# The low-rank tile of a mixture-of-experts kernel: six matmuls and two gelus, or four matmuls and one

## The reference

```
h = gelu(buf @ w1 + b1);  y = h @ w2 + b2          # 256 -> 1024 -> 256
a = gelu(buf @ wd) @ wu                            # 256 -> 32 -> 256, the low-rank branch
y = y + a                                          # weighted, added to the token's row
sh = gelu(xt @ sw1 + sb1) @ sw2 + sb2 + gelu(xt @ swd) @ swu     # shared expert, all tokens
out = out + 0.2 * sh
```

## Time and profile before

| | |
|---|---|
| median of three runs | 178.74 us (177.51 to 179.64) |
| the profiled execution | 177.45 us, span 175.6 us |
| TensorE matmuls busy | 169.9 us, 97%, 1442 matmuls |
| VectorE busy | 144.1 us, 82% |
| ScalarE busy | 140.5 us, 80% |
| GpSimd busy | 96.8 us, 55% |
| chain that ended last | TensorE 93%, DMA 5% |
| mean granted clock of TensorE | 0.999 |

### The profile page before, as it was taken

One profiled execution on the slowest core, in us unless ns is written; L12 is line 12 of the kernel. 1 busy time (PEld: TensorE's weight loads), 2 busy tenths in 40 slices (PEclk: granted clock), 3 DMA queues, 4 the chain that ended last, 5 costly groups with the idle time before them and its releaser, 6 DMA issues.

```text
span 175.6 us, 4118 instructions
## 1 busy us (share of the span) xinstructions
PE 169.9 (97%) x1442; PEld 164.3 (94%) x1442; DVE 144.1 (82%) x330; ACT 140.5 (80%) x315; POOL 96.8 (55%) x112
## 2 busy tenths in 40 slices
PE   5799999999999999999999999999999999999994
PEld 5666879999999999999999999999999999999993
DVE  3478999998695889989889699798988989889722
ACT  3277789407888998997899799999899999897920
POOL 5835348511547572097678858868837555074700
PEclk9999999999999999999999999999999999999999
DMA  4599100069929484595987768769778598776242
GB/s 127 163 350 349 41 2 4 7 175 299 362 56 318 103 304 111 194 252 79 307 252 117 275 193 157 213 197 234 194 255 185 144 312 164 247 247 78 30 90 67
DMA packets 25981, 31.84 MB, mean 181 GB/s; under 512 B 4668, under 2 KB 22488, under 8 KB 25960
## 3 DMA queue, kind: packets, MB, share of 16 engines
q1 hardware_dynamic: 21816, 26.22, 46.7%
q0 software_dynamic: 3904, 5.25, 17.0%
q10 hardware_dynamic: 240, 0.10, 0.2%
HBM read 26.31 MB, written 5.24 MB: 180 GB/s over the span
## 4 chain that ended last, share of the span: by engine, by line
PE 93%; DMA 5%; SPq 0%; DVE 0%; issue 0%; DVEq 0%
PE y_ps L1056 14%; PE y_ps L1057 14%; PE y_ps L1058 14%; PE hid_ps L1056 10%; PE hid_ps L1057 10%; PE hid_ps L1058 10%; DMA x_in<-in_x 5%; PE turn_ps L1056 4%; PE turn_ps L1058 4%; PE turn_ps L1057 4%; PE turn_ps L1235 3%; PE row_ps L1251 1%; PE hid_ps L1095 1%; PE y_ps L1195 1%; PE y_ps L1215 1%; PE y_ps L1251 0%
## 5 line engine op out<-in xcount | busy, mean ns | idle before, releaser
L495 POOL DMA_INDIRECT out_rows<-y_row,slot_tok x23 | 38.5, 1675 | 26.8 <-DVE y_row L946 11.6
L481 POOL DMA_INDIRECT slot_in<-slot_rows,slot_src x23 | 29.5, 1281 | 17.0 <-issue 6.1
L1056 PE MATMUL y_ps<-w_h,hid_h 128*128 128x256 f32 (+2 forms) x128 | 36.4, 285 | 0.0
L1057 PE MATMUL y_ps<-w_l,hid_h 128*128 128x256 f32 (+2 forms) x128 | 36.1, 282 | 0.0
L1058 PE MATMUL y_ps<-w_h,hid_l 128*128 128x256 f32 (+2 forms) x128 | 36.1, 282 | 0.0
L741 DVE TENSOR_TENSOR hid_l<-gelu_f,hid_h 128x320 fp32r<-128x320 f32 (+3 forms) x54 | 26.5, 500 | 8.0 <-ACT hid_h L643 7.5
L1056 PE MATMUL hid_ps<-xs_h,w_h 128*128 128x248 f32 (+6 forms) x96 | 27.6, 288 | 0.0
L1058 PE MATMUL hid_ps<-xs_h,w_l 128*128 128x248 f32 (+6 forms) x96 | 27.2, 284 | 0.0
L1057 PE MATMUL hid_ps<-xs_l,w_h 128*128 128x248 f32 (+6 forms) x96 | 27.2, 284 | 0.0
L718 DVE TENSOR_TENSOR w_l<-w_raw,w_h 128x512 fp32r<-128x512 f32 x40 | 26.7, 703 | 0.0
L643 ACT ACTIVATE hid_h<-hid_ps,bias_s 128x320 fp32r<-128x320 f32 (+2 forms) x48 | 26.4, 549 | 0.0
(11 more groups left out here) (260 smaller groups left out, 465.9 us busy)
## 6 DMA issues: line engine op xcount, KB each, us to landing
w_raw<-in_L_ffn_w SPq DMA_DIRECT2D x16, 1024.0 KB
w_raw<-in_L_ffn_sw SPq DMA_DIRECT2D x3, 1024.0 KB
x_in<-in_x SPq DMA_DIRECT2D x2, 512.0 KB, 4.1
w_raw<-in_L_ffn_sw SPq DMA_DIRECT2D x2, 512.0 KB, 6.5
slot_rows<-token_row SPq DMA_DIRECT2D x8, 128.0 KB, 5.1
wu_raw<-in_L_ffn_wu SPq DMA_DIRECT2D x24, 32.0 KB
out_rows<-base SPq DMA_DIRECT2D x1, 512.0 KB
slot_in<-slot_rows,slot_src POOLq DMA_INDIRECT x23
```

Source lines behind the costliest of these rows:

```text
L481: pool.indirect_dma_start(out=slot_in[par][0:n, s, :], out_offset=None, in_=x_rows, in_offset=bass.IndirectOffsetOnAxis(ap=slot_src[0:n, e ...
L495: pool.indirect_dma_start(out=out, out_offset=bass.IndirectOffsetOnAxis(ap=slot_tok[0:n, e, s:s + 1].bitcast(U32), axis=0), in_=y_row[0:n, ...
L1056: pe.matmul(out_ap, l_h, r_h, start=start, stop=False)
L1057: pe.matmul(out_ap, l_h, r_l, start=False, stop=False)
```

## The change

The low-rank tile of the routed experts takes four matmuls. Its stationary operand `wd_s` holds the high part twice and the low part twice (4 x 32 columns), so that each of `xs_h` and `xs_l` passes once for each of the two halves of the inputs; the bank then has the high-part products on partitions 0 to 63 and the low-part products on 64 to 127. ScalarE copies the upper half out (`low_copy`), VectorE adds the two halves (`low_sum`), ScalarE takes one gelu of the sum in float32 (`low_gelu_part`, behind the gelus of tile 2), and VectorE rounds it by a copy and subtracts the rounded from the unrounded for the low part (`low_lo`, behind the split of tile 2).

The tile is moved: for expert 0 it stands where it stood, for the others it is issued inside the last output tile of the expert before, ahead of its last three matmuls (`LOW_MADE_AT`). The bank `turn_ps[0]` is awaited for tile 5 by the sum. The two slot copies of an expert on ScalarE become one over both banks, and so do the two subtractions on VectorE. On GpSimd the wd cast comes ahead of the gathers. The shared expert's low-rank tile is as before.

```diff
-        turn_ps = [bank(f"turn_ps{i}") for i in range(2)]
+        turn_both = ctx.enter_context(nc.psum_tensor("turn_both", [P, KD, 512], F32))
+        turn_ps = [turn_both[:, k, :] for k in range(KD)]
-        wd_h = [sb(f"wd_h{i}", [P, KD, 3, RANK], F32R) for i in range(2)]
-        wd_l = [sb(f"wd_l{i}", [P, KD, 3, RANK], F32R) for i in range(2)]
+        wd_s = [sb(f"wd_s{i}", [P, KD, 4, RANK], F32R) for i in range(2)]
+        low_sums = gelu_f[0:2 * RANK, 0:2, SLOTS:SLOTS + SLOTS // 2]
...
GpSimd:
             def period(e, par):
+                if e + 2 <= E:
+                    wd_hi_part(e + 2, par)
                 if e + 2 < E:
                     gather(e + 2, par)
-                if e + 2 <= E:
-                    wd_hi_part(e + 2, par)
                 wu_hi_part(e + 2, par)
...
ScalarE:
+            def low_copy(e):
+                act.wait_ge(low_made, e + 1)
+                act.activation(low_sums, halves(turn_ps[0][2 * RANK:4 * RANK, 0:SLOTS]), ACT.Copy).then_inc(low_copied, 1)
+            def low_gelu_part(e):
+                act.wait_ge(low_summed, e + 1)
+                act.activation(low_sums, low_sums, ACT.Gelu).then_inc(low_gelu, 1)
             def slots_hi_part(n):
-                for k in range(KD):
-                    act.activation(xs_h[:, k, 0:n], turn_ps[k][:, 0:n], ACT.Copy).then_inc(slots_hi, 1)
+                act.activation(xs_h[:, :, 0:n], turn_both[:, :, 0:n], ACT.Copy).then_inc(slots_hi, 1)
...
-                for j in range(HT):
+                low_copy(e)
+                for j in range(1, HT):
                     gelu_tile(e + 2, j, MOST[e], lambda f: bias_s[:, e, f:f + 1])
+                    if j == LOW_GELU_AT:
+                        low_gelu_part(e)
...
VectorE:
             def slots_lo_part(e):
                 n = MOST[e]
-                for k in range(KD):
-                    dve.wait_ge(slots_hi, e * KD + (k + 1))
-                    dve.tensor_tensor(xs_l[:, k, 0:n], turn_ps[k][:, 0:n], xs_h[:, k, 0:n].bitcast(F32),
-                                      ALU.subtract).then_inc(slots_lo, 1)
+                dve.wait_ge(slots_hi, e + 1)
+                dve.tensor_tensor(xs_l[:, :, 0:n], turn_both[:, :, 0:n], xs_h[:, :, 0:n].bitcast(F32),
+                                  ALU.subtract).then_inc(slots_lo, 1)
...
+            def low_sum(e):
+                dve.wait_ge(low_copied, e + 1)
+                dve.tensor_tensor(low_sums, halves(turn_ps[0][0:2 * RANK, 0:SLOTS]), low_sums, ALU.add).then_inc(low_summed, 1)
+            def low_lo(e):
+                dve.wait_ge(low_gelu, e + 1)
+                if e > 0:
+                    dve.wait_ge(low_used, e)
+                dve.tensor_copy(halves(low_s[0:2 * RANK, 0:SLOTS]), low_sums).then_inc(low_round, 1)
+                dve.wait_ge(low_round, e + 1)
+                dve.tensor_tensor(halves(low_s[2 * RANK:LOW, 0:SLOTS]), low_sums[0:RANK, :, :],
+                                  halves(low_s[0:RANK, 0:SLOTS].bitcast(F32)),
+                                  ALU.subtract).then_inc(low_split, 1)
...
-                for j in range(HT):
+                low_sum(e)
+                for j in range(1, HT):
                     split_tile(e + 2, j, MOST[e])
+                    if j == LOW_GELU_AT:
+                        low_lo(e)
...
TensorE:
+            def low_tile(e, par, size):
+                pe.wait_ge(slots_lo, e + 1)
+                pe.wait_ge(wd_lo, e + 2)
+                for k in range(KD):
+                    both = wd_s[par][:, k, :, :].rearrange("p g r -> p (g r)")
+                    pe.matmul(turn_ps[0][:, 0:size], both, xs_h[:, k, 0:size], start=(k == 0), stop=False)
+                    ins = pe.matmul(turn_ps[0][:, 0:size], both, xs_l[:, k, 0:size], start=False, stop=(k == KD - 1))
+                ins.then_inc(low_made, 1)
...
+                    if m == KD - 1 and f == LOW_MADE_AT:      # expert_out; rows_out likewise in its last tile
+                        midway()
...
-                    pe.wait_ge(slots_lo, (e + 1) * KD)
-                    for j in range(HT):
+                    if e == 0:
+                        low_tile(0, other, size)
+                    for j in range(1, HT):
                         hidden(e + 2, j, other, e + 1, xs_h, xs_l, slice(0, size), size)
```

More of the change, by code:

```diff
@@ L52 @@
 RING = 5
+LOW_GELU_AT = 2
+LOW_MADE_AT = 7
 MOST = [min(SLOTS, K * T // (r + 1)) for r in range(E)]
@@ L249, in build @@
         wu_lo = sem("wu_lo")
+        low_made = sem("low_made")
+        low_copied = sem("low_copied")
+        low_summed = sem("low_summed")
+        low_gelu = sem("low_gelu")
+        low_round = sem("low_round")
+        low_split = sem("low_split")
+        low_used = sem("low_used")
         hid_made = sem("hid_made")
@@ L284, in hid_count @@
         def hid_count(u, j):
-            return u * HT + (j + 1) - (1 if u == LAST else 0)
+            return u * HT + (j + 1) if u < 2 else 2 * HT + (u - 2) * NF + j
         def turned_part(g):
@@ L334, in held_by @@
         def held_by(u, j):
-            tiles = [i for i in range(1 if u == LAST else 0, j) if hid_banks(u)[i] is hid_banks(u)[j]]
+            tiles = [i for i in range(0 if u < 2 else 1, j) if hid_banks(u)[i] is hid_banks(u)[j]]
             return tiles[-1] if tiles else None
@@ L1140, in hidden @@
                     pe.wait_ge(wd_lo, v + 1)
-                if u < 2 and j == 0:
                     return shared_low(u, x_h, x_l, cols, n)
@@ L1144, in hidden @@
                     pe.wait_ge(hid_gelu, hid_count(u, held_by(u, j)))
+                elif 2 <= u < LAST and hid_bank(u, j) is turn_ps[0]:
+                    pe.wait_ge(low_summed, u - 1)
                 elif u == 1:
                     pe.wait_ge(hid_gelu, hid_count(0, HT - 1))
-                m = P if j > 0 else LOW
-                dst = hid_bank(u, j)[0:m, 0:n]
+                dst = hid_bank(u, j)[:, 0:n]
                 for k in range(KD):
-                    if j == 0:
-                        l_h, l_l = (w[:, k, :, :].rearrange("p g r -> p (g r)") for w in (wd_h[par], wd_l[par]))
-                    else:
-                        l_h, l_l = (w[:, k, (j - 1) * P:j * P] for w in (w1_h[par], w1_l[par]))
+                    l_h, l_l = (w[:, k, (j - 1) * P:j * P] for w in (w1_h[par], w1_l[par]))
                     ins = three(dst, l_h, l_l, x_h[:, k, cols], x_l[:, k, cols], k == 0, k == KD - 1)
@@ L1180, in shared_out, with expert_out @@
                 ins.then_inc(y_made, 1)
-            def expert_out(e, m, par, size):
+            def low_tile(e, par, size):
[6 more added lines that the diff above has]
+                ins.then_inc(low_made, 1)
+            def expert_out(e, m, par, size, midway):
                 v = e + 1
@@ L1193, in expert_out @@
                 cols = slice(m * P, (m + 1) * P)
-                pe.wait_ge(hid_split, hid_count(e + 2, 0))
-                pe.matmul(dst, wu_s[par][:, cols], low_s[:, 0:size], start=True, stop=False)
+                pe.wait_ge(low_split, e + 1)
+                ins = pe.matmul(dst, wu_s[par][:, cols], low_s[:, 0:size], start=True, stop=False)
+                if m == KD - 1:
+                    ins.then_inc(low_used, 1)
                 for f in range(NF):
+                    if m == KD - 1 and f == LOW_MADE_AT:
+                        midway()
                     if m == 0:
@@ L1201, in expert_out, with rows_out @@
                 ins.then_inc(y_made, 1)
-            def rows_out(e, par, size):
+            def rows_out(e, par, size, midway):
                 v = e + 1
@@ L1214, in rows_out @@
                     cols = slice(s * P, s * P + n)
-                    pe.matmul(dst, low_s[:, cols], wu_s[par][:, :], start=True, stop=False)
+                    ins = pe.matmul(dst, low_s[:, cols], wu_s[par][:, :], start=True, stop=False)
+                    if s == tiles[-1]:
+                        ins.then_inc(low_used, 1)
                     for f in range(NF):
+                        if s == tiles[-1] and f == LOW_MADE_AT:
+                            midway()
                         if s == tiles[0]:
@@ L1229, in turn_slots @@
                 else:
-                    pe.wait_ge(slots_lo, e * KD)
+                    pe.wait_ge(slots_lo, e)
                 for k in range(KD):
@@ L1316, in experts, with next_low @@
                         turn_slots(e + 1, other, (sizes[e + 1] + P - 1) // P)
+                    def next_low(e=e):
+                        if e < E - 1:
+                            low_tile(e + 1, e % 2, sizes[e + 1])
                     if e < ROWS_FROM:
                         for m in range(KD):
-                            expert_out(e, m, other, size)
+                            expert_out(e, m, other, size, next_low)
                     else:
-                        rows_out(e, other, size)
+                        rows_out(e, other, size, next_low)
                 last_quarter()
```

18 lines of the change are left out of this document (10 added, 8 removed).

## The result

The kernel after takes **180.13 us** in the median of 20 runs (177.96 to 183.94), the kernel before beside it 178.35 (177.28 to 183.56). Some executions of either kernel are over 1.5% longer than its fastest, whatever the edit, and every ratio here leaves these out: it is **1.0065, 95% interval 1.0034 to 1.0097**. The prediction was 177.1, faster by 0.9%, with 179.2 as its upper end. The change makes the kernel slower by about 1.2 us. The profiled execution has a span of 176.8 us beside 175.6 before.

A forecast was written before the change was run, and what follows sets the result against it. TensorE, busy 97% of the span, was taken as the bound. -1.95 + 0.15 + 0.2 = -1.6 us takes the profiled 177.45 to 175.85; with 1.29 for the median, 177.1 us, range 175.4 to 179.2, chance 0.60.

The forecast's parts named there:

- TensorE, -1.95: Low tiles of eight experts: four matmuls in place of six take a third off 5.86 us, -1.95 us.
- The first expert, +0.15: Expert 0's start: merged slot copy and subtraction can't overlap, so TensorE starts later once, +0.15 us (0 to +0.25).
- VectorE's work: VectorE, per expert: added sum and rounding copy less savings on slots and wd part, net +0.7 us (+0.5 to +0.9).
- VectorE's cover: VectorE's waiting for ScalarE, 1.2 us per expert, covers the added 0.7; tightest hand-over, expert 6, keeps 0.3 us slack.
- Rival (a): Slots' low part, experts 4 to 7: TensorE waits 0.2 to 0.3 us each; gain 0.7, time 178.0 us; chance 0.22.
- (b): VectorE's rounding copy and GpSimd's gathers hold each other; slower, 183.3 us at a whole gather issue; chance 0.10.
- (c): Expert 0's small stalls vanish through ScalarE's earlier copy, nothing else comes: -2.2 us, 176.5 us; chance 0.08.
- Near misses, +0.2: Experts 0 and 5, such as TensorE's turning of the slots into tile 5's bank: +0.2 us in all (0 to +0.6).
- ScalarE's late gelu: Behind tile 2, waiting for VectorE's sum: 0.5 us wait in expert 1, elsewhere the sum is in time; no cost.
- GpSimd, nothing: The wd cast ahead of the gathers, its load late in experts 1 and 6 (4.3 us of waiting): costs nothing.
- The end: Sums' read-back before TensorE's last matmul: up to 0.7 us later, 0.4 of 1.1 us of cover remain; costs nothing.

The follow-up runs named there:

- a10_bank_apart: Kernel after, TensorE's wait for the weighting made by bank (output tiles of experts 5 to 7), VectorE's wait for the combine by row buffer; ratio 0.9931.
- a1_weigh_first: Kernel after, from expert 5 on VectorE weights the previous expert's rows right behind its new low-tile sum, ahead of hidden splits 1 to 3; ratio 1.0100.
- a2_gather_first: Kernel after with GpSimd's wd cast put back behind the gathers, as in the kernel before; ratio 1.0074.
- a7_both: Kernel after with TensorE's wait by bank (output tiles of experts 5 to 7) and the weighting ahead of the split of hidden tile 3; ratio 0.9911.
- a6_weigh_ahead: Kernel after with VectorE's weighting moved ahead of the split of hidden tile 3, for all experts; ratio 1.0020.

## Why the prediction was wrong

**TensorE, -1.95: right,** 1.90. 16 matmuls fewer, spacing unchanged (0.12 us at 248 columns). Without the waits the saving is there: a10_bank_apart ends its matmuls 0.99 us before the kernel before, with 0.89 us more excess at expert 0.

**The first expert, +0.15: right,** 0.16. The merged copy took 0.71 (0.70 said), the subtraction 0.82 (0.81):

```profile
51.60 0.71 ACT L666 ACTIVATE xs_h<-turn_both 128x640 fp32r<-128x640 f32 x1 [0.78 <-PE turn_both L1293]
...
52.34 0.82 DVE L945 TENSOR_TENSOR xs_l<-turn_both,xs_h 128x640 fp32r<-128x640 f32 x1
```

**VectorE's work: right for each instruction.** The groups after (mean ns behind the bar):

```profile
L1030 DVE TENSOR_TENSOR gelu_f<-turn_both,gelu_f 64x320 f32<-64x320 f32 x8 | 3.8, 479 | 0.8 <-ACT gelu_f L658 0.8
L1037 DVE CAST low_s<-gelu_f 64x320 fp32r<-64x320 f32 x8 | 2.5, 316 | 0.0
L1039 DVE TENSOR_TENSOR low_s<-gelu_f,low_s 32x320 fp32r<-32x320 f32 x8 | 4.5, 561 | 0.3
```

The copy is 0.32 us, not 0.35, and the sum 0.48, within 0.40 to 0.48. The Trainium skill (VectorE: DVE Perf Modes, on the perf-mode tiers) gave an estimated 0.32 for a float32 copy within SBUF; the trace agrees. VectorE's busy time as a whole rose by 3.6 us, not 5.

**VectorE's cover: the step that failed.** The prediction said that the cover is VectorE's waiting for ScalarE, "1.2 us per expert, of which I fill 0.7", and that "what counts is the tightest hand-over", which it put at expert 6's slots and last split, with 0.3 us to spare. The rule was right and the list of hand-overs was short: it left out the third one, the weighting, which stands behind the split of tile 3 and ahead of the output tiles. Its slack in the kernel before was 0.15 us at expert 5, 142.94 against 143.28 or 0.34 at expert 6, and 155.22 against 155.32 or 0.10 at expert 7. It was the tightest of all. And the 1.2 us of idling was no cover for it: at the splits of tiles 7 and 8, 0.14 and 0.34 us in expert 4, it lies behind the weighting, and of the 0.63 us ahead of it in expert 5 (0.23, 0.09, 0.31) VectorE, which needs ScalarE's tiles there, could fill but half (0.29 left after). Nor did VectorE move up with TensorE, as the prediction had it ("so they move up too"): at expert 5 TensorE comes 0.55 us sooner and the weighting ends 0.37 later. Measured from where TensorE would start its output, the weighting ends 0.92, 0.82 and 0.93 us later than before at experts 5, 6 and 7; less the slack that is 0.77, 0.48 and 0.83. With the 0.24 at expert 3 that is some 2.4 us (2.37 in the table), where the forecast had 0. The wait is in the code quoted ahead of the prediction (`y_weighted` in `rows_out`).

**Rival (a), half given back by VectorE being late:** right in kind, VectorE late against TensorE, and wrong in place and size. It had the slots' low part ahead of the low tile; nothing stands there in experts 4 to 7. **(b), the rounding copy held by GpSimd:** wrong as to its size. In expert 0 the copy ran from 57.23 beside the gather of 56.98 and took 0.31; it was never over 0.36 in the profile after. In other kernels it was longer at times, 0.49 beside a gather (a10_bank_apart at 86.36), up to 0.58 beside a gather and a cast (a1_weigh_first at 100.19); that is 0.27 over its usual 0.31, under the 0.33 of waiting that (b) needed. What GpSimd does hold is VectorE's subtractions, and it is its casts that do it, not its gathers: the one behind the copy took 0.68 where it met the cast of 58.10, and 0.48 beside a gather alone (127.63). Over all 16 traces, of the 128x320 splits beside gathers or combines alone none of 549 took over 0.60 us, beside a cast 30 of 90. The Trainium skill (SBUF — State Buffer, on who interferes with whom) has it that a VectorE instruction with two SBUF inputs contends with a GpSimd one that reads SBUF, and that against VectorE in a two-port mode the shared port is held for whole instructions. The first agrees with these subtractions, and with the split of 0.74 that the prediction put to the two-port mode; for this copy beside this gather of 1.11 us no hold shows. **(c):** wrong, expert 0 lost more, not less.

**Near misses, +0.2:** 0.68 at expert 0, not from the ScalarE order that was priced but from TensorE's late signals, part of it perhaps luck; 0.12 at the turning of the slots in expert 5, which is within its 0.85. **ScalarE's late gelu** waited nowhere that cost. **GpSimd, nothing:** its waiting for the wd load rose from 4.3 to 16.1 us after 52 us,

```profile
POOL wd_s L472 <- DMA wd_raw<-in_L_ffn_wd: 16.1, 5, 9.0
```

and a2_gather_first shows that it costs no measurable time, though GpSimd's cast of wu, which now meets the split of tile 3, is part of the gap of expert 5. **The end:** the sums are back at 173.32, before the last matmul (173.96), with 0.6 us of cover left where 0.4 was said.

## What to carry to other kernels

When an engine on the bound is sped up, list every wait in its program, not those that the profile shows, and put a slack on each: a wait with 0.1 us to spare has no row. Idle time of the helper engine is cover only if it lies ahead of the hand-over, so sum it up to there. And where a wait covers several buffers, wait for the one that is needed: it cost nothing here (0.9997 on the kernel before), and the kernel after went from 1.0065 to 0.9931 of the kernel before with both waits made finer (a10_bank_apart).

## What was not expected of the hardware

- TensorE's signals can reach ScalarE late and in a bunch while GpSimd writes indirect gathers: three signals of tiles 0.79 us apart came within 0.15 us, up to 1.9 us late, and with the gathers taken away or moved they don't (one trace each). The kernel before has signals 1.0 us late there too. TensorE's own records show nothing of it. The Trainium skill (Perfetto Trace Analysis, on what the profiler-reported window captures) says that a semaphore's propagation lies outside of an instruction's record; the trace agrees. Whether the signals are held at TensorE or on their way no run here shows.
- TensorE's granted clock halved after a stand of 1.88 us and stayed so for 3.4 us, after 143 us of full clock (a7_both). A stand of 1.46 us (a6_weigh_ahead at 59.86) was not followed by it.
- A cast on GpSimd can lengthen VectorE's subtraction beside it from 0.48 to 0.68 us; an indirect gather alone did not in any of the traces.
- The combine's landing varies by microseconds: in the profile of a7_both VectorE stood for it four times, 8.6 us in all and 4.8 at the longest, in that of a10_bank_apart never. It is a ring, weighting to combine to landing to weighting, and how much of the long runs it sets stays open.
